# Layer norm in front of windowed attention: mean by a matrix that carries the group norm's scale, shift carried as a bias to the square and to the last scaling

## What is computed

```python
x = x + _L0_conv_ref(_gn(x), ...)      # windowed attention + MLP with a depthwise conv, 16x16 windows, step 14
x = x + _L1_conv_ref(_gn(x), ...)      # clustering layer

def _gn(v, G=32, eps=1e-5):            # group norm, no weights: mean and variance of 3 channels x H x W
    g = v.reshape(B_, G, C_ // G, H_, W_)
    m = jnp.mean(g, axis=(2, 3, 4), keepdims=True)
    s = jnp.var(g, axis=(2, 3, 4), keepdims=True)
    return ((g - m) / jnp.sqrt(s + eps)).reshape(v.shape)

# at the head of _L0_conv_ref, for every token (pixel) of every window:
y = _layernorm(tok, norm1_w, norm1_b)  # over the 96 channels, eps 1e-5
q, k, v = y @ wq, y @ wk, y @ wv       # then attention in each window
```

## Time and profile before

| | us |
|---|---|
| median of 3 runs | 7700.91 |
| lowest, highest | 7690.25, 7706.97 |
| the profiled execution's own time | 7690.68 |
| its span in the trace | 7688.9 |
| the `layer_norm` stage in it (first load issued 169.57, next stage's first transfer 637.07) | 467.5 |

### The profile page before, as it was taken

The page is one execution under the profiler, slowest core; times in us unless marked ns, Lnnn a source line. Parts: engine busy times, 40 slices in busy tenths (PEclk is TensorE's granted clock), DMA queues, the critical chain, the costliest instruction groups (busy, mean ns, idle before and its releaser), DMA issues. The chain is left out here.

```text
span 7688.9 us, 138214 instructions
## 1 busy us (share of the span) xinstructions
PE 6602.4 (86%) x52604; PEld 3232.1 (42%) x52604; DVE 4890.2 (64%) x7370; ACT 3553.5 (46%) x5600; POOL 2457.7 (32%) x3173
## 2 busy tenths in 40 slices
PE   0886999999999999999997898899957768688885
PEld 0332555555555555555553333555500000476662
DVE  6785777777777777777774555788812222454554
ACT  0553666666666666666664666344401101243330
POOL 0443444444444444444445565000012222000000
PEclk9997999999999999999998999999988989787885
DMA  7784333334333434333325886988799999345655
GB/s 300 196 239 124 77 77 78 88 85 91 79 71 73 88 83 92 83 77 77 78 46 155 254 250 206 359 342 344 282 249 274 248 272 250 97 112 140 172 147 164
DMA packets 480460, 1252.80 MB, mean 163 GB/s; under 512 B 159620, under 2 KB 164740, under 8 KB 442628
## 3 DMA queue, kind: packets, MB, share of 16 engines
q1 hardware_dynamic: 444276, 1141.72, 54.3%
q0 software_dynamic: 7168, 50.34, 2.1%
q10 hardware_dynamic: 28368, 51.91, 1.8%
HBM read 731.14 MB, written 458.07 MB: 155 GB/s over the span
## 5 line engine op out<-in xcount | busy, mean ns | idle before, releaser
L727 DVE TENSOR_REDUCE at_mz<-at_ps 128x4 bf16<-128x1024 f32 x1444 | 1774.6, 1229 | 782.5 <-PE at_ps L651 782.2
L600 ACT ACTIVATE at_E<-at_ps 128x1024 f32<-128x1024 f32 x1444 | 1500.9, 1040 | 794.7 <-PE at_ps L663 794.7
L663 PE MATMUL at_ps<-at_qaug,at_k 32*128 32x256 f32 x11552 | 830.0, 401 | 79.2 <-DVE at_qaug L751 79.2
L674 PE MATMUL at_ps<-at_E,at_vaug 128*32 128x256 f32 x11552 | 774.3, 386 | 0.0
L1190 PE MATMUL cv_ps<-cv_yin,cv_band 128*128 128x384 f32 x2304 | 745.4, 486 | 27.9 <-DMA cv_yin<-y_mlp 27.9
L1210 DVE TENSOR_TENSOR cv_yin<-cv_gl,cv_yin 64x384 f32<-64x384 f32 x1152 | 637.5, 553 | 150.8 <-ACT cv_gl L1201 142.9
L663 PEld LDWEIGHTS at_ps<-at_qaug,at_k 32*128 32x128 f32 x11552 | 523.1, 184 | 443.1 <-issue 224.5
L1297 POOL TENSOR_TENSOR f_xa<-f_xa,f_xb 128x3840 f32<-128x3840 f32 (+1 forms) x28 | 213.2, 7636 | 1544.1 <-DMA f_xb<-in_x 1544.1
L540 POOL TENSOR_TENSOR at_share<-at_rden,t_share 128x8 f32<-128x8 f32 x722 | 146.8, 203 | 1558.8 <-DVE at_rden L738 1558.6
L1336 DVE SCALAR_TENSOR_TENSOR f_xa<-f_ps,f_b,f_xa 128x512 f32<-128x512 f32 (+1 forms) x216 | 136.2, 687 | 753.6 <-PE f_ps L1320 753.6
L1317 PE MATMUL f_ps<-f_sa,f_wa 128*32 128x512 f32 (+1 forms) x1728 | 379.8, 958 | 268.2 <-DMA f_sbb<-s_mlp 268.2
(11 more groups left out here) (210 smaller groups left out, 9570.2 us busy)
## 6 DMA issues: line engine op xcount, KB each, us to landing
cv_yin<-y_mlp SPq DMA_DIRECT2D x48, 2340.0 KB, 14.7
s_mlp<-cv_yin SPq DMA_DIRECT2D x48, 2340.0 KB, 8.4
at_rows_in<-y_attention SPq DMA_DIRECT2D x38, 1536.0 KB, 9.4
gn_xin<-in_x SPq DMA_DIRECT2D x16, 3072.0 KB, 23.2
ln_xin<-in_x SPq DMA_DIRECT2D x192, 256.0 KB, 7.6
y_attention<-ln_xin SPq DMA_DIRECT2D x192, 256.0 KB, 3.8
cl_xu<-x SPq DMA_DIRECT2D x128, 384.0 KB, 3.8
cl_xv<-x SPq DMA_DIRECT2D x64, 768.0 KB, 5.5
```

The lines of the kernel that those rows point to most:

```text
L600: act.activation(E[:, m % 2, 2 * p:2 * p + 2, :], psum[:, 2 + 2 * p:4 + 2 * p, :], ACT.Exp).then_inc(exp_done, 1)
L663: i = pe.matmul(psum[:, 2 + h, TOK * j:TOK * j + TOK], k[rows, n % 2, tokens(w, 128 * j, 128)], qaug[rows, m % 2, :], start=True, stop=True)
L674: i = pe.matmul(pv_ps[32 * h:32 * h + VC, 0:TOK], vaug[:, m % 2, z, h, :], E[:, m % 2, h, z * TOK:(z + 1) * TOK], start=(z == 0), stop=(z ...
L727: dve.tensor_reduce(mz[:, m % 2].rearrange("p j (h c) -> p h j c", c=32)[:, 2 * p:2 * p + 2, :, DQ], psum[:, 0:2, :].rearrange("p h (j n) ...
```

## The change

In `layer_norm`:

- The Identity pass of ACT is gone. The mean is taken from the raw image: DVE builds once `mixed`, three 128 x 128 matrices, `ones` times a channel's scale, and `mean` multiplies the loaded chunk by them. A tile's load is now waited for by PE.
- `centred` is now s x - mean(s x), by three instructions (scalar_tensor_tensor) of 512 elements with the scale as the per-partition scalar.
- What is left of the shift is h - mean(h), built once: three matmuls of `ones` with the shift (128 x 1), a copy `total`, and a subtraction give `bias`.
- The square moves from POOL to ACT: three Square activations of 512 elements with `bias` as bias, in ACT's order at the place where the Identities stood. POOL has nothing to do in the stage.
- `normalised` is (chunk + bias) x rs, by three scalar_tensor_tensor of 512 elements.
- The semaphores are renamed and joined; Ln and Exp count on one (`rs_done`).

In `cluster` seven semaphores become two (`lhs_steps`, `lhs_taken`) that count the same events in the same order; no instruction and no wait for data is added or moved.

```diff
         @block.tensor
         def _(pe):
             pe.wait_ge(w_loaded, 16 * (2 * MOVES + 1))
+            for grp in range(CGRP):
+                m = pe.matmul(psum[:, 2, 0:1], ones[:], shift[:, grp:grp + 1], start=(grp == 0), stop=(grp == CGRP - 1))
+            m.then_inc(total_done, 1)
+            pe.wait_ge(mixed_done, CGRP)
+            pe.wait_ge(bias_done, 1)
 
             def mean(n):
-                pe.wait_ge(xh_done, n + 1)
+                if n % PER == 0:
+                    pe.wait_ge(loaded[n // PER % XB], 16 * MOVES * (n // PER // XB + 1))
                 if n >= 2:
                     pe.wait_ge(cen_done, n - 1)
                 for grp in range(CGRP):
-                    m = pe.matmul(psum[:, n % 2, :], ones[:], chunk(n, grp), start=(grp == 0), stop=(grp == CGRP - 1))
+                    m = pe.matmul(psum[:, n % 2, :], mixed[:, grp, :], chunk(n, grp), start=(grp == 0), stop=(grp == CGRP - 1))
                 m.then_inc(mean_done, 1)
...
+            mean(0)
+            for n in range(N):
+                if n + 1 < N:
+                    mean(n + 1)
+                variance(n)
...
+            def square(n):
+                act.wait_ge(cen_done, n + 1)
+                if n >= 2:
+                    act.wait_ge(var_done, n - 1)
+                for grp in range(CGRP):
+                    m = act.activation(sq[:, n % 2, grp], chunk(n, grp), ACT.Square, bias=bias[:, grp:grp + 1])
+                m.then_inc(sq_done, 1)
+
+            act.wait_ge(bias_done, 2)
             for k, i, a, b in slots():
                 if a is not None:
-                    if i == 0:
-                        act.wait_ge(loaded[k % XB], 16 * MOVES * (k // XB + 1))
-                    for grp in range(CGRP):
-                        m = act.activation(chunk(a, grp), chunk(a, grp), ACT.Identity, bias=shift[:, grp:grp + 1], scale=scale[:, grp:grp + 1])
-                    m.then_inc(xh_done, 1)
+                    square(a)
                 if i == 1 and 1 <= k <= NT:
                     act.wait_ge(var_out, k * PER)
                     r = rs[:, (k - 1) % 3, :]
-                    act.activation(r, r, ACT.Ln, bias=t["eps5"][:]).then_inc(log_done, 1)
-                    act.wait_ge(log_done, k)
+                    act.activation(r, r, ACT.Ln, bias=t["eps5"][:]).then_inc(rs_done, 1)
+                    act.wait_ge(rs_done, 2 * k - 1)
                     act.activation(r, r, ACT.Exp, scale=-0.5).then_inc(rs_done, 1)
...
+            dve.wait_ge(w_loaded, 16 * (2 * MOVES + 1))
+            for grp in range(CGRP):
+                dve.tensor_scalar(mixed[:, grp, :], ones[:], scale[:, grp:grp + 1], None, ALU.mult).then_inc(mixed_done, 1)
+            dve.wait_ge(total_done, 1)
+            dve.tensor_copy(total[:], psum[:, 2, 0:1]).then_inc(bias_done, 1)
+            dve.wait_ge(bias_done, 1)
+            dve.tensor_scalar(bias[:], shift[:], total[:, 0:1], None, ALU.subtract).then_inc(bias_done, 1)
+            dve.wait_ge(bias_done, 2)
 
             def normalised(n):
-                dve.wait_ge(rs_done, n // PER + 1)
-                dve.tensor_tensor(chunk(n), chunk(n), over_groups(rs[:, n // PER % 3, cols(n)]), ALU.mult).then_inc(z_done, 1)
+                dve.wait_ge(rs_done, 2 * (n // PER + 1))
+                for grp in range(CGRP):
+                    m = dve.scalar_tensor_tensor(out=chunk(n, grp), in0=chunk(n, grp), scalar=bias[:, grp:grp + 1], in1=rs[:, n // PER % 3, cols(n)],
+                                                 op0=ALU.add, op1=ALU.mult)
+                m.then_inc(z_done, 1)
 
...
+                for grp in range(CGRP):
+                    m = dve.scalar_tensor_tensor(out=chunk(n, grp), in0=chunk(n, grp), scalar=scale[:, grp:grp + 1], in1=psum[:, n % 2, :],
+                                                 op0=ALU.mult, op1=ALU.subtract)
+                m.then_inc(cen_done, 1)
```

More of the change, by code:

```diff
@@ L238, in layer_norm @@
         ones = sb("ones", [128, 128])
-        scale, shift = sb("scale", [128, CGRP]), sb("shift", [128, CGRP])
+        mixed = sb("mixed", [128, CGRP, 128])
+        scale, shift, bias = sb("scale", [128, CGRP]), sb("shift", [128, CGRP]), sb("bias", [128, CGRP])
+        total = sb("total", [128, 1])
         psum = ctx.enter_context(nc.psum_tensor("ln_ps", [128, 4, 512], F32))
@@ L243, in layer_norm @@
         stored = [sem(f"stored{i}") for i in range(XB)]
-        xh_done, mean_done, cen_done, sq_done, var_done, var_out, log_done, rs_done, z_done = (
-            sem(n) for n in ("xh_done", "mean_done", "cen_done", "sq_done", "var_done", "var_out", "log_done", "rs_done", "z_done"))
+        mixed_done, total_done, bias_done, mean_done, cen_done, sq_done, var_done, var_out, rs_done, z_done = (
+            sem(n) for n in ("mixed_done", "total_done", "bias_done", "mean_done", "cen_done", "sq_done", "var_done", "var_out", "rs_done", "z_done"))
         block = ctx.enter_context(nc.Block())
@@ L290, in _ @@
                 sp.wait_ge(stored[i], 16 * MOVES * len(range(i, NT, XB)))
[L292 to L298, removed]
         @block.tensor
@@ L1630, in cluster @@
         rt_done, sim_done, sg_done, sm_done, chain = sem("rt_done"), sem("sim_done"), sem("sg_done"), sem("sm_done"), sem("chain")
-        tp_done, tp_out, agg_done, agg_read, comb_done, den_done, aggn_done, at_done, at_out, lhs_done, lhs_out = (
-            sem(n) for n in ("tp_done", "tp_out", "agg_done", "agg_read", "comb_done", "den_done", "aggn_done", "at_done", "at_out", "lhs_done", "lhs_out"))
+        tp_done, tp_out, agg_done, agg_read, den_done, lhs_steps, lhs_taken = (
+            sem(n) for n in ("tp_done", "tp_out", "agg_done", "agg_read", "den_done", "lhs_steps", "lhs_taken"))
         y_done, y_out = sem("y_done"), sem("y_out")
@@ L1762, in piece @@
                 if i == 0:
-                    pe.wait_ge(lhs_out, f + 1)
+                    pe.wait_ge(lhs_taken, 3 * f + 3)
                 if order(f, i):
@@ L1880, in normalised @@
             def normalised(f):
[L1881 removed]
+                dve.wait_ge(lhs_steps, 3 * f + 1)
                 dve.tensor_scalar(den[:], turn_ps[:, C:VC], 1.0, None, ALU.add).then_inc(den_done, 1)
@@ L1886, in normalised @@
                 dve.wait_ge(den_done, 3 * f + 3)
-                dve.scalar_tensor_tensor(out=agg[:], in0=agg[:], scalar=den[:, 0:1], in1=t["own_channels"][:], op0=ALU.mult, op1=ALU.mult).then_inc(aggn_done, 1)
+                dve.scalar_tensor_tensor(out=agg[:], in0=agg[:], scalar=den[:, 0:1], in1=t["own_channels"][:], op0=ALU.mult, op1=ALU.mult).then_inc(lhs_taken, 1)
             def columns(f):
-                dve.wait_ge(at_done, f + 1)
-                dve.tensor_copy(aggt[:], turn_ps[0:C, 0:128]).then_inc(at_out, 1)
+                dve.wait_ge(lhs_steps, 3 * f + 2)
+                dve.tensor_copy(aggt[:], turn_ps[0:C, 0:128]).then_inc(lhs_taken, 1)
             def weights(f):
-                dve.wait_ge(lhs_done, f + 1)
-                dve.tensor_copy(lhs[:, f % 2, :], turn_ps[:, 0:C]).then_inc(lhs_out, 1)
+                dve.wait_ge(lhs_steps, 3 * f + 3)
+                dve.tensor_copy(lhs[:, f % 2, :], turn_ps[:, 0:C]).then_inc(lhs_taken, 1)
             def added(f, i):
```

21 lines of the change are left out of this document (6 added, 15 removed).

## The result

The median of the changed kernel is 7666.47 us (7654.78 to 7687.07, 14 runs), that of the kernel before 7702.77 us (7675.86 to 7718.26, 14 runs): 36 us less. The ratio estimated from the runs is 0.996 (31 us) with a 95% interval from 0.9947 to 0.9973, that is 21 to 41 us. The profiled execution has a span of 7666.0 us.

What follows compares the result with a forecast made beforehand. DVE was taken as fullest, slowed beside POOL, with PE the floor under it. Period 3 x 5.15 + 7.7 + 1.1 = 24.3 us put the next stage at 605.3 instead of 637.07: 32 us gained, forecast 7666, range 7641 to 7689.

Steps and rivals of the forecast that it cites:

- What bounds it, and POOL's part: In layer_norm DVE is fullest, 23.4 us per tile; beside POOL's multiplication its two-SBUF-operand instruction stalls, some 1.7 us per chunk.
- Three for one on DVE: Three 512-element instructions replace one large: 2.0 us per group against 1.69; DVE 18.4 us per tile instead of 23.4.
- Square: Square with bias on ACT, 512 elements: 0.72 us each, ends 0.63 and 0.80; three take 2.0 us.
- The regular chunk: In chunks without Ln and Exp the square is ready 0.75 us early, so PE alone sets 5.15 us.
- The chunk with Ln and Exp: Once per tile ACT's Ln and Exp delay the square: 7.7 us instead of 5.15, PE idles 2.4.
- The clock: After PE's gap the product may run at the lower clock: two thirds of 1.7, 1.1 us per tile.
- Head: Start of layer_norm, up to tile 0 normalised: at 251.0 instead of 259.54, 8.5 us earlier.
- Tail: End of layer_norm, from tile 13 normalised to the next stage: 38.4 us, against 37.8 before.
- Loads: Load seen 25.4 us after the store began, wanted after 29.2: 3.8 us to spare; transfers about 23.3 us per tile.
- rival 2: Faster than forecast: no low clock, Square at 0.63, period falls to the transfers' 23.3; 47 us gained, 7644; chance 0.06.
- A drain behind each table load: Skill's rule adding about 1.38 us per ACT table load, 2.8 us more per tile; prediction said the trace disagrees.
- The gaps of the kernel before: PE's gaps of 2.31 and 2.80 us before the change were put down to Ln and Exp delaying the Identities.

Runs made afterwards that it cites:

- e4_pool_square: The changed kernel with the squares put back on POOL, one multiplication per chunk, bias left out of the square: 7719.6 us, ratio 1.0015 to the kernel before.
- e5_one_multiply: The changed kernel with the last scaling as one multiplication of 1536 elements, bias left out of it: 7665.1 us, ratio 0.9942 to the kernel before.
- e3_split: The changed kernel with Exp moved one slot down, so Ln follows the second square and Exp the third: 7642.3 us, ratio 0.9916 to the kernel before.
- e1_ln_only: The kernel before with the change in layer_norm alone, cluster keeping its eleven old semaphores: 7667.1 us, ratio 0.9951 to the kernel before.
- e7_split_ahead5: e3_split with loads issued five tiles ahead instead of four: 7618.6 us, ratio 0.9893 to the kernel before.
- e9_before_ahead5: The kernel before with loads issued five tiles ahead instead of four: 7691.2 us, ratio 0.9975 to the kernel before.
- e10_after_ahead5: The changed kernel with loads issued five tiles ahead instead of four, Ln and Exp left together: 7675.7 us, ratio 0.9951 to the kernel before.

## Why the prediction held

The forecast was 7666 us and the measured median is 7666.5. The mechanism held, but the agreement to 0.5 us is luck. The stage's gain was put 7.5 us too low (32 against 39.5). Against that, the forecast of 7666 stands for a kernel before of 7698, and its median over 14 runs is 7702.8, 5 more; the rest, some 3 us, is the difference between 39.5 us in the stage and 36 in the medians.

- *What bounds it, and POOL's part.* Right, and shown by e4_pool_square: 4.18 us against 2.07, with DVE busy all the time and the gain gone.
- *Three for one on DVE.* Taken at 0.66 us from start to start with both operands in SBUF, from a row with PSUM; a group took 2.07. Both groups together cost 0.6 us more per chunk than the large instructions, as counted. Hidden under PE, as said (shown for one of the two groups by e5_one_multiply).
- *Square.* 0.72 forecast, 0.710 measured; no table load of its own (32 in the stage, two per tile, as before).
- *The regular chunk.* 5.15 us, set by PE, as said; the square was done 0.9 us early where 0.75 was forecast.
- *The chunk with Ln and Exp.* A gap of 2.4 us was forecast, 2.22 came: three squares take 1.95 us, not 2.0, and each stands a tenth earlier. From one variance product's start to the next this is 7.53 us (242.98 to 250.51) where 7.7 was forecast; 0.1 comes back in the product behind the gap. That the block on ACT makes the gap is shown by e3_split, in which it vanishes.
- *The clock.* Two thirds of the gaps were to be followed by the long product; it is 7 of all 15, and every second one in the body. This is the mis-sized term of the period: 0.85 us per tile instead of 1.1, 4 of the 5.6 us by which the body was put too long. The period is 23.93 instead of 24.3.
- *Head.* 251.0 forecast, 248.46 measured. The first square was done when expected (variance product at 194.05, forecast 193.8), but that product took 2.84 us and not the 4.43 that I had carried over from the earlier trace rows, and there was no low clock behind the first gap. The latter can fall otherwise: in e1_ln_only the first gap had the long product behind it, and the first store came at 251.22.
- *Tail.* 38.4 forecast, about 38.8 measured.
- *Stage.* 39.5 us were gained, not 32. The median's gain is 36 (interval 21 to 41), so nothing need have been lost elsewhere; in the profiled pair 16.6 were, 14.1 of them in `cluster` along with PE's lower mean clock.
- *Loads.* PE waited for none but the first, as said. But the "23.3 us without the ends" that I took for the transfers' floor, the end of rival 2 and a bound of the range, was no floor: e7_split_ahead5 moves the same bytes in 20.6. The step that failed is reading a floor off this stretch: in the kernel before the DMA engines were busy for only 0.92 of it, at 259 GB/s. That alone leaves 24.3 x 0.92 = 22.4 us. The rest is the rate itself, which a busy share of about 1 does not fix: within one tile of e7_split_ahead5 it went from 434 GB/s, where the tile's stores end and loads begin, to 225. Why it differs so is not shown. The windows view of the kernel before, then of e7_split_ahead5:

```profile
389.70:414.00 24.30, 20.28 (x43) 8.38 (x42) 20.53 (x12) 15.04 (x16) 9.86 (x4) 0.93 0.92 259
```

```profile
398.00:400.00 2.00, 2.00 (x6) 0.95 (x5) 1.50 (x4) 1.82 (x3) 0.00 (x0) 1.00 1.04 434
404.00:406.00 2.00, 2.00 (x6) 0.95 (x5) 2.00 (x4) 1.98 (x4) 0.00 (x0) 1.00 0.96 225
```

- *A drain behind each table load (the Trainium skill, "ScalarE: Activation LUTs", "What ACT_TABLE_LOAD costs").* The traces do not agree with it here: in e3_split Ln starts at 304.67, as its table load of 1.28 us from 303.38 ends, and the changed kernel's tiles take 23.09 us where the clock stays up, which leaves no room for 2.8 more.
- *The gaps of the kernel before.* The prediction put PE's gaps of 2.31 and 2.80 us down to the block of Ln and Exp alone. e9_before_ahead5, in which the later ones are all 2.3, shows that what exceeds 2.3 was the loads' doing, with 0.5 us per tile and some at the ends. This did not bend the forecast, since the new end of the stage was built up from the changed kernel's own steps and the old one was measured; it changes only what the gain is put down to.

## What to carry to other kernels

Look at two instructions of the same shape with different durations first: here the slower one had both operands in SBUF and overlapped GpSimd, and the overlap was lost. Then ask where the moved work goes; here each half of the change alone (off GpSimd, or one pass fewer) lost time, and only both together gained. A block that an engine does once per tile costs what is longer than the slack of the chunk around it, so splitting it into pieces that fit the idle time between two chunks can be worth nearly as much as the change itself (24 us here, by e3_split, against 36). It moves the bound on to the lead of the loads, which is one number. And try that number on the kernel before as well: there it gave 11.8 us of the stage without the change.

## What the hardware showed unexpectedly

- A constant gap of 2.22 us on PE was followed by the lower clock exactly every second time over the last 14 of the stage's 15 gaps, in the changed kernel and again in e10_after_ahead5; in e1_ln_only it was so from the first gap on.
- The same instructions of `cluster` took 1032 to 1067 us in 12 traces, with DVE, ACT and POOL busy for the same 524 to 525, 314 and 33 us each time. From a single pair of traces no difference below some 30 us can be read there.
- Loads and stores of 8 KB rows together ran at 309 GB/s for 100 us (e7_split_ahead5, share 1.00), well over the 237 of the earlier trace rows at a share of 0.85. A share near 1 went with anything from 225 to 434 GB/s, so it is not by itself a sign that the transfers are at their limit.
